# Neighbourhood attention: the gate's first layer with pixels stationary and its second on VectorE, the row sums spread by GpSimd, and input fetches and the values' store issued by GpSimd

## The reference

```python
qkv = (x @ qkv_w + qkv_b).reshape(B, H, W, 3, HEADS, HEAD_DIM)      # 4 heads of 32
scores = einsum('bxyhd,bxyklhd->bxyhkl', q, kwin) + bias            # 7 x 7 window of keys
attn_out = einsum('bxyhkl,bxyklhd->bxyhd', softmax(scores), vwin) @ proj_w + proj_b
gate = sigmoid(relu(x @ g1_w + g1_b) @ g2_w + g2_b)                 # 128 -> 64 -> 1 per pixel
return attn_out * gate + x
```

## Time and profile before

| | |
|---|---|
| three runs, us | 4094.99, 4100.4, 4109.84; median 4100.4 |
| profiled execution, us | 4106.21 |
| its span, first to last instruction, us | 4104.3 |
| mean granted TensorE clock | 0.944 |
| busy over the span: TensorE, VectorE, ScalarE, GpSimd, us | 3848.4, 3178.8, 2742.7, 1252.4 |
| first layer's loop over blocks | about 28 to 648 us of the span |

### The profile page before, as it was taken

The page is one execution under the profiler, slowest core; times in us unless marked ns, Lnnn a source line. Parts: engine busy times, 40 slices in busy tenths (PEclk is TensorE's granted clock), DMA queues, the critical chain, the costliest instruction groups (busy, mean ns, idle before and its releaser), DMA issues. The chain is left out here.

```text
span 4104.3 us, 73691 instructions
## 1 busy us (share of the span) xinstructions
PE 3848.4 (94%) x25466; PEld 3005.5 (73%) x25466; DVE 3178.8 (77%) x7667; ACT 2742.7 (67%) x6175; POOL 1252.4 (31%) x1311
## 2 busy tenths in 40 slices
PE   8999997999999999999999999988799995888898
PEld 5777775899888998889988899976566662333347
DVE  5888886777787777877778777759566677998885
ACT  5777775677777777767777667658643437777753
POOL 3444443000010000100001000006124467888873
PEclk8999998999999999999999999999899995777789
DMA  7766661000010000100001000013223335556557
GB/s 191 188 177 174 175 164 46 18 19 23 18 43 26 19 23 18 43 26 19 23 18 41 18 13 11 9 44 109 89 99 135 135 147 188 179 182 210 167 193 230
DMA packets 306380, 374.50 MB, mean 91 GB/s; under 512 B 41306, under 2 KB 172378, under 8 KB 305242
## 3 DMA queue, kind: packets, MB, share of 16 engines
q1 hardware_dynamic: 291754, 351.70, 27.9%
q0 software_dynamic: 12672, 17.71, 1.6%
q10 hardware_dynamic: 1584, 0.40, 0.1%
HBM read 197.00 MB, written 119.54 MB: 77 GB/s over the span
## 5 line engine op out<-in xcount | busy, mean ns | idle before, releaser
L944 ACT ACTIVATE l_ph<-l_T 128x512 fp32r<-128x512 f32 x1024 | 612.4, 598 | 547.6 <-PE l_T L849 547.6
L1061 DVE TENSOR_TENSOR l_pl<-l_T,l_ph 128x512 fp32r<-128x512 f32 x1024 | 707.6, 691 | 274.8 <-ACT l_ph L944 274.1
L1050 DVE CUSTOM_DVE_ANT_0 l_pr<-l_S,l_zero 128x512 f32<-128x512 f32 x1024 | 705.1, 689 | 74.5 <-PE l_S L772 11.7
L949 ACT ACTIVATE l_pr<-l_pr,l_st 128x512 f32<-128x512 f32 x1024 | 731.6, 714 | 1.1 <-DVE l_st L1056 1.0
L861 PE MATMUL l_O<-l_ph,l_vh 128*128 128x256 f32 x2048 | 661.7, 323 | 12.3 <-DVE l_pl L1061 12.2
L849 PE MATMUL l_T<-l_ident,l_pr 128*128 128x128 f32 x4096 | 612.8, 272 | 0.0
L849 PEld LDWEIGHTS l_T<-l_ident,l_pr 128*128 128x128 f32 x4096 | 507.7, 140 | 136.3
L862 PE MATMUL l_O<-l_ph,l_vl 128*128 128x256 f32 x2048 | 577.9, 282 | 0.0
L863 PE MATMUL l_O<-l_pl,l_vh 128*128 128x256 f32 x2048 | 577.1, 282 | 0.0
L1093 POOL TENSOR_TENSOR l_xs<-l_xs,l_bob 128x128 f32<-128x128 f32 x128 | 57.3, 461 | 1644.1 <-DMA l_xs<-x 1643.2
L770 PE MATMUL l_S<-l_kh,l_qh 128*128 128x512 f32 x1024 | 417.0, 407 | 0.5 <-DVE l_kl L1010 0.2
(11 more groups left out here) (265 smaller groups left out, 8104.7 us busy)
## 6 DMA issues: line engine op xcount, KB each, us to landing
l3b_u<-ub SPq DMA_DIRECT2D x256, 256.0 KB, 3.0
l_kq<-l_hl SPq DMA_DIRECT2D x372, 128.0 KB, 3.2
zs<-l_tmp SPq DMA_DIRECT2D x64, 256.0 KB, 2.2
ub<-l3a_u SPq DMA_DIRECT2D x32, 512.0 KB, 3.3
l3b_z<-zs SPq DMA_DIRECT2D x64, 256.0 KB, 3.5
yz<-l3b_z SPq DMA_DIRECT2D x64, 256.0 KB, 3.3
l3b_dt<-yz SPq DMA_DIRECT2D x32, 512.0 KB, 5.3
l_vg<-vs SPq DMA_DIRECT2D x256, 55.0 KB
```

The lines of the kernel that those rows point to most:

```text
L944: e.activation(ph[:, i, :], psT[:, i, :], ACT.Copy).then_inc(p_hi, 1)
L949: e.activation(pr[:, s, es], pr[:, s, es], ACT.Exp, bias=st[:, s, 9:10], scale=SC, accum_out=st[:, s, 10 + k:11 + k]).then_inc(exped, 1)
L1050: e.tensor_tensor_reduce(pr[:, s, ks], psS[:, bk, :], zero[:].broadcast_to([128, 512]), 1.0, -3.0e38, ALU.add, ALU.max, st[:, s, kc:kc + 1 ...
L1061: e.tensor_tensor(pl[:, i, :], psT[:, i, :], f32(ph[:, i, :]), ALU.subtract).then_inc(p_lo, 1)
```

## The change

Five things change, all in `layer0`:

- The gate's first layer is computed with the pixels stationary: four matmuls of 128 pixels against the 64 columns of `g1w` give 128 pixels x (4 x 64) in `psP`. VectorE adds the bias `g1b`, then does maximum with 0 and product with `g2w` in one instruction, and sums over the 64 with a reduction; these are the gate's four columns, from which ScalarE takes the exponential as before. ScalarE's Relu and TensorE's second layer in `turn` (and, for the first two groups, ahead of the loop) go. `psP` is now freed by VectorE for this job.
- The reciprocals of the row sums are widened from 4 to 128 columns by GpSimd (`widen`, new tile `rx`, new semaphore `spread`), and one 128 x 128 matmul against the identity takes the place of the four small ones.
- The input is also laid out in the blocks' order on the host (`xB`), and fetched into a tile of its own, `xq`, for queries and the gate; `xn` serves keys and values. Both have two slots, where `xn` had three.
- `fetch` (now `fetch_rows` and `fetch_blocks`) and `keep_v` move from SP's queue to GpSimd's. In each block of GpSimd the order is: `widen`, `base`, the store of the result, the next fetch of `x`, then the moved DMAs of that block's job.
- The fetch of `x` has six slots in place of seven.

```diff
-        g2w = P.sb("g2w", [64, 1])
+        g1b, g2w = P.sb("g1b", [128, 64]), P.sb("g2w", [128, 64])
...
-        xn = P.sb("xn", [128, 3, 512])
+        xn = P.sb("xn", [128, 2, 512])
+        xq = P.sb("xq", [128, 2, 512])
         vst = P.sb("vst", [128, 2, 512])
-        gt = P.sb("gt", [64, 512])
+        gt = P.sb("gt", [128, 256])
...
+        rx = P.sb("rx", [128, 2, 128])
...
-        xs = P.sb("xs", [128, 7, 128])
+        xs = P.sb("xs", [128, 6, 128])
...
             w = Waits(e)
+
+            def fetch_rows(G):
+                b, rb = divmod(G, 8)
+                if G >= 2:
+                    for what in ("k", "v"):
+                        full(w, (what, G - 2))
+                e.dma_start(xn[:, G % 2, :], io["xT"][b, :, 512 * rb:512 * rb + 512]).then_inc(xn_in[G % 2], 16)
+
+            def fetch_blocks(G):
+                b, rb = divmod(G, 8)
+                if G >= 2:
+                    for what in ("q", "hide"):
+                        full(w, (what, G - 2))
+                e.dma_start(xq[:, G % 2, :], io["xB"][b, :, 512 * rb:512 * rb + 512]).then_inc(xq_in[G % 2], 16)
+
+            def keep_v(G):
+                b, rb = divmod(G, 8)
+                emptied(w, ("v", G))
+                e.dma_start(vs[b, 8 * rb:8 * rb + 8].rearrange("(t r) c d -> (r c) t d", r=2), vst[:, G % 2, :].rearrange("p (t c) -> p t c", t=4)).then_inc(v_out[G % 4], 16)
 
             def bring(n):
                 b, r0, c0, _, _ = where(n)
-                if n >= 7:
-                    w.wait_ge(y_done, n - 6)
-                e.dma_start(xs[:, n % 7, :], io["x"][b, r0:r0 + 8, c0:c0 + 16, :]).then_inc(xs_in[n % 7], 16)
+                if n >= 6:
+                    w.wait_ge(y_done, n - 5)
+                e.dma_start(xs[:, n % 6, :], io["x"][b, r0:r0 + 8, c0:c0 + 16, :]).then_inc(xs_in[n % 6], 16)
 
             def base(n):
 
...
-                w.wait_ge(xs_in[n % 7], 16 * (n // 7 + 1))
-                e.tensor_tensor(xs[:, n % 7, :], xs[:, n % 7, :], tg[:, n % 2, :], ALU.add).then_inc(based, 1)
-
+                w.wait_ge(xs_in[n % 6], 16 * (n // 6 + 1))
+                e.tensor_tensor(xs[:, n % 6, :], xs[:, n % 6, :], tg[:, n % 2, :], ALU.add).then_inc(based, 1)
+
+            def widen(n):
+
+                w.wait_ge(summed, n + 1)
+                if n >= 2:
+                    w.wait_ge(R_full, n - 1)
+                e.tensor_copy(rx[:, n % 2, :].rearrange("p (h c) -> p h c", h=4),
+                              st[:, n % 4, 12:16].rearrange("p (h a) -> p h a", a=1).broadcast_to([128, 4, 32])).then_inc(spread, 1)
+
+            for G in range(2):
+                fetch_rows(G)
+                fetch_blocks(G)
             bring(0)
             stack(e, w, 1, ("k",), k1_in)
+            fetch_rows(2)
+            keep_v(0)
+            keep_v(1)
+            fetch_blocks(2)
+            fetch_rows(3)
             for n in range(N + 6):
+                if 0 <= n - 3 < N:
+                    widen(n - 3)
                 if 0 <= n - 2 < N:
                     base(n - 2)
                 if 0 <= n - 5 < N:
...
                 if n + 1 < N:
                     bring(n + 1)
+                for what, G in jobs(n):
+                    if what == "v":
+                        keep_v(G)
+                        if G + 2 < NB:
+                            fetch_rows(G + 2)
+                    elif what == "hide" and G + 2 < NB:
+                        fetch_blocks(G + 2)
+                if n == 0:
+                    fetch_blocks(3)
             for i in range(3):
                 w.wait_ge(y_out[i], 16 * len(range(i, N, 3)))
...
+                s = G % 2
                 if (what, G) in early:
                     bank, done = early[what, G], early_full
                 else:
                     bank, done = psP[:], P_full
                     if p_use[what, G]:
                         w.wait_ge(P_free, p_use[what, G])
-                if what in ("q", "k"):
-                    w.wait_ge(xn_in[s], 16 * (G // 3 + 1))
+                if what in ("q", "hide"):
+                    w.wait_ge(xq_in[s], 16 * (G // 2 + 1))
+                else:
+                    w.wait_ge(xn_in[s], 16 * (G // 2 + 1))
+                if what == "q":
                     w.wait_ge(prepared, 3)
-                    if what == "q":
-                        e.matmul(bank, wqkv[:, 0:128], blocks(xn[:, s, :]), start=True, stop=True).then_inc(done, 1)
-                    else:
-                        e.matmul(bank, wqkv[:, 128:256], xn[:, s, :], start=True, stop=True).then_inc(done, 1)
+                    e.matmul(bank, wqkv[:, 0:128], xq[:, s, :], start=True, stop=True).then_inc(done, 1)
+                elif what == "k":
+                    w.wait_ge(first, 32)
+                    e.matmul(bank, wqkv[:, 128:256], xn[:, s, :], start=True, stop=True).then_inc(done, 1)
                 elif what == "v":
-                    w.wait_ge(xn_in[s], 16 * (G // 3 + 1))
                     w.wait_ge(first, 32)
                     for k in range(4):
                         t = e.matmul(bank[:, 128 * k:128 * k + 128], xn[:, s, 128 * k:128 * k + 128], wqkv[:, 256:384], start=True, stop=True)
                     t.then_inc(done, 1)
-                elif what == "hide":
-                    w.wait_ge(xn_in[s], 16 * (G // 3 + 1))
+                else:
                     w.wait_ge(weights, 128)
-                    e.matmul(bank[0:64, :], g1w[:], blocks(xn[:, s, :]), start=True, stop=True).then_inc(done, 1)
-                else:
-                    w.wait_ge(P_free, p_use["hide", G] + 1)
                     for k in range(4):
-                        t = e.matmul(bank[:, k:k + 1], gt[:, 128 * k:128 * k + 128], g2w[:], start=True, stop=True)
+                        t = e.matmul(bank[:, 64 * k:64 * k + 64], xq[:, s, 128 * k:128 * k + 128], g1w[:], start=True, stop=True)
                     t.then_inc(done, 1)
 
...
-                G = opening(n + 2) if h == 0 else None
-                if G is not None:
-                    w.wait_ge(P_free, p_use["hide", G] + 1)
-                    for k in range(4):
-                        e.matmul(psT[:, 0, 384 + k:385 + k], gt[:, 128 * k:128 * k + 128], g2w[:], start=True, stop=True)
                 w.wait_ge(exped, v + 1)
                 for j, (o, m) in enumerate(((0, 110), (110, 110), (220, 88))):
...
                     if n >= 4:
                         w.wait_ge(y_done, n - 3)
-                    for h in range(4):
-                        t = e.matmul(psF[32 * h:32 * h + 32, 0:128], st[:, (n - 3) % 4, 12 + h:13 + h].broadcast_to([128, 32]), ident[:],
-                                     start=True, stop=True, tile_position=(0, 32 * h))
-                    t.then_inc(R_full, 1)
+                    e.matmul(psF[:, 0:128], rx[:, (n - 3) % 2, :], ident[:], start=True, stop=True).then_inc(R_full, 1)
 
...
-                elif what == "hide":
-                    full(w, (what, G))
+                elif what == "open":
                     w.wait_ge(prepared, 4)
-                    e.activation(gt[:], psP[0:64, :], ACT.Relu, bias=cols[0:64, 3:4]).then_inc(P_free, 1)
-                elif what == "open":
-                    full(w, (what, G))
-                    e.activation(gate[:, 0, 4 * G:4 * G + 4], psP[:, 0:4], ACT.Exp, bias=cols[:, 4:5], scale=-1.0).then_inc(P_free, 1)
+                    w.wait_ge(opening_in, G + 1)
+                    e.activation(gate[:, 0, 4 * G:4 * G + 4], gate[:, 0, 4 * G:4 * G + 4], ACT.Exp, bias=cols[:, 4:5], scale=-1.0).then_inc(opened_out, 1)
 
...
                                     bvb[:].rearrange("p (a c) -> p a c", a=1).broadcast_to([128, 4, 128]), ALU.add).then_inc(free, 1)
+                elif what == "hide":
+                    t, per = gt[:].rearrange("p (k c) -> p k c", k=4), lambda v: v.rearrange("p (a c) -> p a c", a=1).broadcast_to([128, 4, 64])
+                    full(w, (what, G))
+                    w.wait_ge(weights, 128)
+                    e.tensor_tensor(t, bank[:, 0:256].rearrange("p (k c) -> p k c", k=4), per(g1b[:]), ALU.add).then_inc(free, 1)
+                    w.wait_ge(P_free, p_use[what, G] + 1)
+                    e.scalar_tensor_tensor(t, t, 0.0, per(g2w[:]), ALU.max, ALU.mult).then_inc(weighted, 1)
+                    w.wait_ge(weighted, G + 1)
+                    e.tensor_reduce(gate[:, 0, 4 * G:4 * G + 4], t, AX.X, ALU.add).then_inc(opening_in, 1)
                 elif what == "open":
                     sl = slice(4 * G, 4 * G + 4)
-                    if G < 2:
-                        emptied(w, (what, G))
-                    else:
-                        w.wait_ge(opened_out, G - 1)
+                    w.wait_ge(opened_out, G + 1)
                     e.tensor_scalar(gate[:, 1, sl], gate[:, 0, sl], 1.0, None, ALU.add).then_inc(gate_den, 1)
                     w.wait_ge(gate_den, G + 1)
...
                 w.wait_ge(exped, 4 * n + 4)
                 if n >= 4:
```

(2 more changed lines are left out.)

48 lines of the change are left out of this document (14 added, 34 removed).

## The result

The changed kernel took 4109.9 us, median of 20 runs (4104.4 to 4118.4), the kernel before, on the same chip between them, 4102.3, median of 20 runs (4095.0 to 4112.5). The ratio is 1.0020, 95% interval 1.0013 to 1.0026: 0.2% slower, which is within the 0.3% called no change. The forecast of 4067 us and its range of 4045 to 4093 are both missed. The profiled execution took 4108.1 us (span 4106.3).

The account below looks back on a forecast made before the run. TensorE's own instructions were taken to set the pace, the stack a close second limit. Terms -0.98 + 0.05 - 0.08 + 0.2 - 0.3 = -1.1 us a group, over 30 groups -33 us, gave 4067 us; range 4045 to 4093.

Parts of the forecast that it names:

- Transfers moved: SP's queue: loses 0.82 us of issue and a store wait, needing 17.0 to 17.3 us a group; -0.3 us a group.
- the -0.3 that I took back: First score of each group: 0.3 of some 0.5 us standing for the stack goes; bounds 0 and -0.6.
- the rival that states it: SP and DMA engines keep the pace: stack's issue stretches by 1 us, group 18.4 us, 4082 us; chance 0.16.
- Second layer off TensorE: Queries' block: the gate's second layer leaves TensorE, -0.98 us a group.
- First layer turned: Gate's block on TensorE: eight load and stream pairs take 1.0 us, +0.05 a group; bounds -0.5 and +0.1.
- VectorE: Gate's block: three new VectorE instructions of 1.25 us together, charged +0.2 us a group; bounds 0 and 1.25.
- the 0.22 us bound: VectorE's product of two SBUF tensors: possible extra 0.22 us, left out of the sum; 6.6 us over 30 groups.
- The spread: Row sums by one full matmul instead of four column tiles: -0.02 us a block, -0.08 a group.
- GpSimd's cover: Wait on `spread`: after GpSimd's widening of 0.45 to 0.62 us, about 3 us remain before TensorE's matmul needs it.
- GpSimd's queue: Slower rival: moved 256 KB DMAs priced by bytes need up to 19.9 us a group, 4125 us; chance 0.08.
- Start and end: Start: SP loses one fetch and two stores, GpSimd gains fetches; within 2 us either way, taken as nothing.

Follow-up runs that it names:

- e8: Changed kernel with the loop's two input fetches issued later in GpSimd's queue, at the keys' and queries' blocks; 4099.6 us, ratio 0.9993 to the kernel before.
- e14: Changed kernel with the third value-window fetch on GpSimd and the loop's input fetches later in GpSimd's queue; 4071.7 us, ratio 0.9919 to the kernel before.
- e15: Kernel before with only the third fetch of each value window moved to GpSimd; 4089.3 us, ratio 0.9961.
- e9: Changed kernel with the third fetch of each value window issued by GpSimd, four a group; 4094.1 us, ratio 0.9975 to the kernel before.
- e4: Kernel before with only the loop's input fetch and values' store moved from SP's to GpSimd's queue; 4091.5 us, ratio 0.9965.
- e7: Kernel before with moved transfers and the gate on VectorE, all jobs reading one block layout, values stored in four 64 KB DMAs, no widening; 4096.2 us, ratio 0.9982.
- e5: Changed kernel without the widening, row sums spread by four column-tile matmuls again; 4101.3 us, ratio 1.0001 to the kernel before.
- e6: Kernel before with only the widening by GpSimd and one full matmul for the spread; 4103.6 us, ratio 1.0003.
- e3: Changed kernel with the first four groups' fetches and first two stores back on SP, loop unchanged; 4112.5 us, ratio 1.0018 to the kernel before.
- e1: Changed kernel with its input fetches and values' store back in SP's queue; 4130.5 us, ratio 1.0065 to the kernel before.

## Why the prediction was wrong

The step that failed is "Transfers moved": "SP loses 0.82 us of issue and the wait for the store behind it: 12 x 0.715 + 8.39 = 17.0, at most 17.3 with the gaps", and with it what follows there: the stack "is then issued as soon as its queries are split and lands 8.4 + 3.2 us later". In the changed kernel the same 24 issues take 9.05 + 9.69 = 18.7 us (means of SP's timeline over the stretch). Three terms are mis-sized. The windows are 0.5 more, and were before too (9.02): 0.715 came from six issues, the mean over the stretch is 0.75. The stack is 1.3 more. Its 8.39 came from a kernel in which GpSimd sends no large transfer (the mean before is 8.54); now its issues of 0.6 us become 0.88, 1.26, 0.85 and 0.87 from 408.98 on, behind GpSimd's store and fetch of 256 KB at 407.96 and 408.77: the part that relieved SP put them there. Even without that, 9.0 + 8.5 = 17.5 would have left next to nothing beside TensorE's 17.65.

The third term is the landing: from its first issue to its last landing the stack takes 14.6 us, not 11.6, and with a full SP it is not issued as soon as the queries are split but 2.5 us behind that, in the mean. So the -0.3 that I took back turned into +0.8 of lateness, the clock's falls in it. The text had the condition ("if SP's air went again, the stack would be late again") and the rival that states it, with 18.4 us a group and 4082; it was right in its mechanism and too cheap, for these terms and for the clock. The cause has two parts, and both are shown: SP's missing air by e8 against e14 and by the kernel before against e15, the collision of GpSimd's large transfers with the stack's issues and landings by e9 against e14. Neither alone was enough to bring the stack in time.

The other terms, against the blocks of groups without standing (values, gate, keys, queries; e4 4.33, 4.44, 4.30, 5.44; e7 4.32, 4.33, 4.51, 4.35; e14 4.33, 4.34, 4.62, 4.35):

*Second layer off TensorE,* -0.98: the queries' block fell by 1.09. Right.

*First layer turned,* +0.05: the gate's block fell by 0.11. In e7 the eight pairs take 0.91 us from their start to the score (403.42 to 404.33), as much as the values' job (416.61 to 417.52) and less than L348's 0.98 that I went by. Half the moving columns gave nothing against the values' job, which speaks for the loads as what sets the time; the Trainium skill's rule on LDWEIGHTS ("TensorE: Matmul & The Clock Gate"), by which eight were 0.85, an estimate, agrees within 0.06.

*VectorE,* +0.2: its three instructions are 1.26 us, as forecast (1.25), and the block behind the gate's is 0.21 longer in e7. Right in size; that this is VectorE's load is argued from the block's place, not shown. The product of two SBUF tensors took 425 ns, the sum from PSUM 414: nothing of the 0.22 us bound. But none of its 29 runs in the stretch fell beside a copy, sum or product of GpSimd, so the rule behind that bound was not put to the test.

*The spread,* -0.08: it is +0.15 to +0.21. Attention product and spread take 1.12 us (407.34 to 408.46) for 1.02. The new matmul starts 0.11 later behind the product and then takes 0.33 us to the next job, as the four tiles did; the streaming I counted on is not there. From each of the four jobs to its first score 0.10 come back (gate: 408.46 to 409.27, against 0.91 in e7), so on TensorE itself the exchange is about even; the loss stands in one or two blocks of a group, as said with e5 and e6, and why is open. GpSimd's cover was right, but for 0.4 us in two waits of TensorE's weight loads on `rx` in 500 us; the side effect on VectorE's copy of the maxima was not seen.

Sum on TensorE: forecast -0.98 + 0.05 - 0.08 + 0.2 = -0.81, measured -0.86. In e14, where the stack is in time, the time is 4071.7, in the forecast's own range; that is in part luck. In its trace the layer's loop is 47 us shorter than before and not 33, mainly because nearly all of the lateness goes and not 0.3 us a group of it, and start, end and the layers behind are 4, 3 and 5 us longer, which the forecast had at nothing.

*GpSimd's queue,* the rival on the slower side: 0.82, 0.59 and 0.57 us for the three 256 KB issues, so by descriptors and cheaper still, and never late. The Trainium skill ("DMA: Bandwidth & Descriptors", section "SWDGE vs HWDGE vs iDMA") prefers SP for plain transfers; this is not borne out here: e4 gains 0.35% by moving them. *Start and end:* the start was "taken as nothing" and is +5.8 us, the end, +3.0, was not in the sum; but e3 shows that the start's part is not missed while the stack is late.

## What to carry to other kernels

A group is not the groups: take the shortest that many share as the engine's own pace, and the mean less that as the price of lateness; from one group that was itself late, both come out wrong. A queue's need is the sum of its issues with the gaps over many groups, and it grew here when large transfers of another queue ran beside it; a transfer moved off the queue is still in its way. Beside the queue's sum, add up the way of the one result that TensorE needs: when its input is ready, how long it waits for the queue, its issues, and its last landing. It must fit in one group, and air on the queue mends only one of these terms. Before work is taken off the engine, give the queue that feeds it air, here by four small fetches a group on another queue: they gained 0.4% on the kernel before, 0.45% on the changed one, and 1.0% there together with later fetches.

## What the runs showed of the hardware

- Issues on SP are not of one length: the same stack DMA took 0.59 to 2.07 us (median 0.64) in the changed kernel, 0.59 to 2.03 (median 0.60) before.
- From the last of twelve issues to the last landing the stack took 2.5 us before, 4.9 in the changed kernel and 3.5 in e14, with DMA shares of 0.66, 0.77 and 0.76: the share does not tell it.
- Long waits of TensorE for the stack were followed by a lower clock. In the changed kernel between 100 and 600 us four waits were: 2.43, 1.93, 2.36 and 2.82 us (at 154, 232, 362 and 570 us), each with 0.83 over the 10 us from it or around it; in the kernel before 2.99 us at 132, with 0.66 over 130 to 140 us, in the group that took 24.69. The length of the wait alone does not decide it: in the changed kernel one of 1.57 us at 58 us was followed by a fall and those of 1.59, 1.63 and 1.68 were not, nor were three of 2.04 to 2.31 us in e8.
- GpSimd's drain at the end of the layer took 1.54 us in the kernel before and in e6, and 3.8 to 5.1 us in all the others. Why is open: in e1, with 4.6 us, GpSimd issues none of the further transfers either.
- GpSimd issued a 256 KB store in 0.82 us and 256 KB fetches in 0.57 to 0.59, the fetches in less time than the 0.61 to 0.68 of its 64 KB transfers.
